# Q, K and V of a 16-head attention: projected token-major and transposed per head by TensorE, with the batch loop written out

## The reference

```python
def _L1_attn_ref(x, Wqkv, Wproj, bproj):
    qkv = jnp.einsum('bnm,fm->bnf', x, Wqkv)          # b=8, n=1024, m=256, f=768
    qkv = qkv.reshape(b, n, N_HEADS, -1)
    q, k, v = (qkv[..., :dh], qkv[..., dh:2 * dh], qkv[..., 2 * dh:])   # dh=16
    scores = jnp.einsum('bnhd,bngd->bnhg', q, k) / SCALE
    attn = jax.nn.softmax(scores, axis=-1)
    out = jnp.einsum('bnhg,bngd->bnhd', attn, v)
    return jnp.einsum('bni,mi->bnm', out.reshape(b, n, -1), Wproj) + bproj
x = L0_attn_x
x = _layernorm(x + _L0_attn_ref(...))
x = _layernorm(x + _L0_ffn_ref(...))
x = _layernorm(x + _L1_attn_ref(...))
x = _layernorm(x + _L1_ffn_ref(...))
```

## Time and profile before

| | us |
|---|---|
| median of 3 runs (lowest, highest) | 1611.36 (1608.79, 1613.42) |
| the profiled execution | 1609.18 |
| its span, first to last instruction | 1607.4 |
| PE, DVE, ACT, POOL busy | 1255.6, 958.1, 669.8, 601.5 |
| mean granted TensorE clock, share of full | 0.837 |
| second transfer queue's total (q1) | 79.93 MB |

### The profile page before, as it was taken

One profiled execution on the slowest core, in us unless ns is written; L12 is line 12 of the kernel. 1 busy time (PEld: TensorE's weight loads), 2 busy tenths in 40 slices (PEclk: granted clock), 3 DMA queues, 4 the chain that ended last, 5 costly groups with the idle time before them and its releaser, 6 DMA issues. The chain is left out here.

```text
span 1607.4 us, 33289 instructions
## 1 busy us (share of the span) xinstructions
PE 1255.6 (78%) x12232; PEld 791.7 (49%) x12232; DVE 958.1 (60%) x2185; ACT 669.8 (42%) x1164; POOL 601.5 (37%) x889
## 2 busy tenths in 40 slices
PE   7689869976998868986898869988789777774452
PEld 4454546543664546553565537545465435531441
DVE  2434666685656747485556756477466866475535
ACT  3322552355432752344623662336523553253423
POOL 2133271344522543335613545324713435243212
PEclk9789977998879977989789887999779886797556
DMA  4000442018120370207320180205520080208220
GB/s 149 14 5 16 102 63 54 15 40 147 16 67 7 95 99 10 59 14 141 47 67 8 66 127 3 66 8 121 72 54 1 27 149 11 54 3 159 24 54 27
DMA packets 92918, 90.78 MB, mean 56 GB/s; under 512 B 7031, under 2 KB 81721, under 8 KB 92474
## 3 DMA queue, kind: packets, MB, share of 16 engines
q1 hardware_dynamic: 90170, 79.93, 25.6%
q0 software_dynamic: 2560, 8.39, 1.5%
HBM read 46.35 MB, written 41.94 MB: 55 GB/s over the span
## 5 line engine op out<-in xcount | busy, mean ns | idle before, releaser
L1430 PE MATMUL bank<-we,at 128*128 128x512 f16 x1536 | 397.3, 423 | 98.0 <-DVE x L1143 49.1
L1430 PEld LDWEIGHTS bank<-we,at 128*128 128x128 f16 x1536 | 161.2, 107 | 317.1 <-issue 126.1
L513 POOL TENSOR_TENSOR part<-part 128x512 f32<-128x512 f32 x64 | 81.2, 1269 | 353.3 <-ACTq L792 353.2
L651 ACT ACTIVATE part<-bank,wexp 128x256 f32<-128x256 f32 x256 | 104.3, 470 | 202.0 <-PE bank L1430 156.9
L768 ACT ACTIVATE x<-x,nm,rs 128x256 f32<-128x256 f32 x192 | 104.4, 593 | 132.5 <-POOL nm L501 132.0
L1143 DVE SCALAR_TENSOR_TENSOR x<-bank,wexp,x 128x256 f32<-128x256 f32 x256 | 122.7, 479 | 56.8 <-PE bank L1430 46.8
L1430 PE MATMUL bank<-bt,wqkv 128*128 128x512 f16 x576 | 138.8, 382 | 20.9 <-DVE stage L985 18.3
L985 DVE TENSOR_TENSOR stage<-bank,stage 128x512 f16<-128x512 f32 x128 | 86.3, 686 | 102.7 <-ACT stage L651 102.7
L651 ACT ACTIVATE blockdiag<-shared,const 128x2048 f16<-128x2048 f16 x64 | 122.7, 1990 | 36.4 <-POOL shared L545 35.6
L651 ACT ACTIVATE stage<-bank 128x512 f16<-128x512 f32 x128 | 75.2, 596 | 125.5 <-PE bank L1430 82.1
L494 POOL TENSOR_SCALAR nm<-mv 128x2 f32<-128x2 f32 x128 | 29.7, 232 | 259.7 <-DVE mv L1020 254.8
(11 more groups left out here) (175 smaller groups left out, 2209.9 us busy)
## 6 DMA issues: line engine op xcount, KB each, us to landing
scratch_qkv<-stage SPq DMA_DIRECT2D x48, 512.0 KB, 3.4
ct<-scratch_qkv SPq DMA_DIRECT2D x128, 128.0 KB, 5.9
x_in<-in_x_dram SPq DMA_DIRECT2D x32, 256.0 KB, 2.7
keys<-scratch_qkv SPq DMA_DIRECT2D x64, 128.0 KB, 10.9
scratch_o<-stage SPq DMA_DIRECT2D x64, 128.0 KB, 3.1
bt<-scratch_o SPq DMA_DIRECT2D x16, 512.0 KB, 3.7
out_dram<-x POOLq DMA_DIRECT2D x32, 256.0 KB, 2.6
blockdiag<-in_expert_w_dram SPq DMA_DIRECT2D x1, 2048.0 KB
```

The costliest lines, as they stand in the source:

```text
L513: pool.tensor_tensor(part[:, 0:2, :], part[:, 0:2, :], part[:, 2:4, :], ALU.add)\
L651: return act.activation(dst, src, ACT.Copy, scale=scale)
L1430: ins = pe.matmul(dst, lhs, rhs, start=(n == 0), stop=(n == len(terms) - 1))
```

## The change

Q, K and V are computed token-major. `b_fqk(b, u)` takes the 128 tokens 8n+u (`x2t`, every eighth column of `bt`) as stationary operand and 512 columns of `wqkv` (Q and K) as moving one, six matmuls; eight of them replace the first eight pieces. `b_fv` does the same for V with 256 columns, twelve matmuls for each of four pairs of tiles. ACT alone copies the fp32 result to SBUF (`qk_tok` in half 1 of `blockdiag`, `v_tok` in `ct`) and frees the bank. Then `b_turn(b, m, j)` transposes four heads of matrix m by TensorE (four fp32 128x128 transposes into one bank), and ACT and DVE split that into operand rows: K straight into `keys`, Q into `bt` (`q_rows`), V into `stage` (`v_rows`). There are 12 such groups in a batch: Q and K at the end of the turn that projects them, V in the next turn between `a_moe` 0, 1 and the first scores. The scratch tensor, its transfers and the four GpSimd copies are gone. The spreads read the new rows. The loops of all five engines are written out for all ten turns.

```diff
-        def f_part(k, part):
-        ...
+        def rows_part(m, j, part):
+            if m == "K":
+                return keys[:, 4 * j:4 * j + 4, P * part:P * (part + 1)]
+            if m == "Q":
+                return q_rows[:, part, :, :, 4 * j:4 * j + 4].rearrange("p c t h -> p h t c")
+            return v_rows[:, part, :, :, 4 * j:4 * j + 4].rearrange("p c u d -> p d (c u)")
+        x2t = bt[:, :, :, :].rearrange("p k l (n u) -> p k l n u", u=T)
# SP: b_f, b_loadq, b_loadk, b_loadv are gone
# POOL
-                pool.tensor_copy(q_rows[hf].rearrange("p (s c) h -> p s c h", c=8),
-                                 compact[:, :, 8 * hf:8 * hf + 8, :]).then_inc(q_turned, 1)
-                pool.tensor_copy(v_rows[hf].rearrange("p (s c) h -> p s c h", c=8),
-                                 compact[:, :, 8 * hf:8 * hf + 8, :]).then_inc(v_turned, 1)
# ACT
-                if k // 2 >= 2:
-                    act.wait_ge(stored[(k // 2) % 2], 48 * b + 16 * (k // 4))
-                copy(f_part(k, HI), f_psum(k)).then_inc(f_hi, 1)
+            def b_fqk(b, u):
+                act.wait_ge(b_full, b_filled(b, f"FQK{u}"))
+                copy(qk_tok[:, :, u, :], b_ps(f"FQK{u}").rearrange("p (m d) -> p m d", d=DH))\
+                    .then_inc(b_free[b_ring(f"FQK{u}")], 1)
+            def b_turn(b, m, j):
+                act.wait_ge(b_full, b_filled(b, f"T{m}{j}"))
+                copy(rows_part(m, j, HI), rows_psum(m, j)).then_inc(turned, 1)
...
                 if c is not None:
-                    b_spreadq(c, slice(0, 5))
+                    b_spreadq(c, slice(0, 3))
                 if b is not None:
                     a_moe(b, 0)
                 if c is not None:
+                    b_turn(c, "V", 0)
+                    b_turn(c, "V", 1)
+                    b_spreadq(c, slice(3, 5))
+                if b is not None:
+                    a_moe(b, 1)
+                if c is not None:
+                    b_turn(c, "V", 2)
+                    b_turn(c, "V", 3)
                     b_spreadq(c, slice(5, T))
# DVE
-                split_lo(f_part(k, LO), f_psum(k), f_part(k, HI)).then_inc(b_free[b_ring(f"F{k}")], 1)
+                split_lo(rows_part(m, j, LO), rows_psum(m, j), rows_part(m, j, HI))\
+                    .then_inc(b_free[b_ring(f"T{m}{j}")], 1)
# PE
+            def b_fqk(b, u):
+                pe.wait_ge(b_free[b_ring(f"FQK{u}")], b_before(b, f"FQK{u}"))
+                if u == 0:
+                    pe.wait_ge(b_free[b_ring("TX3")], b_read(b, "TX3"))
+                sum_of(b_ps(f"FQK{u}"), split_terms(lambda k, i: x2t[:, k, i, :, u],
+                                                    lambda k, j: wqkv[:, j, k, 0:2 * D])).then_inc(b_full, 1)
+            def b_turn(b, m, j):
...
+                for i in range(4):
+                    n = 4 * j + i
+                    if m == "V":
+                        src = v_tok[:, :, :].rearrange("p t (g d) -> p (t g) d", d=DH)[:, :, n]
+                    else:
+                        src = qk_tok[:, H * "QK".index(m) + n, :, :].rearrange("p u d -> p (u d)")
+                    ins = pe.transpose(b_ps(f"T{m}{j}")[:, P * i:P * (i + 1)], src, ident)
+                ins.then_inc(b_full, 1)
...
-                    b_f(b, 10)
+                    b_fv(b, 2)
+                    b_fv(b, 3)
+                    b_turn(b, "Q", 0)
+                    b_turn(b, "Q", 1)
                 if a is not None:
                     a_gate(a)
                 if b is not None:
-                    b_f(b, 11)
+                    b_turn(b, "Q", 2)
+                    b_turn(b, "Q", 3)
                 if a is not None:
                     a_wt(a)
-                    a_bias(a, 0)
...
+                for p in range(TP):
+                    if b is not None:
+                        b_turn(b, "K", p)
+                    if a is not None:
+                        a_bias(a, p)
# every engine
-            with pe.Fori(2, NB) as i:
+            for i in range(2, NB):
                 turn(i, i - 1, i - 2)
```

More of the change, by code:

```diff
@@ L324, in build_two_layer_postln @@
         out_d = out.rearrange("b (t p) d -> b p t d", p=P)
-        q_src, k_src, v_src = [scratch_qkv[D * n:D * (n + 1)].rearrange("(h d) (r n) -> h d r n", d=DH, r=T)
-                               for n in range(3)]
         def places():
@@ L435, in b_loado, with turn @@
                         .then_inc(o_loaded, 16)
-            def turn(a, b, c):
+            def turn(a, c):
                 if c is not None:
@@ L442, in turn @@
                         load_x(a, p)
-                if b is not None:
-                    b_f(b, 1)
-                    b_f(b, 3)
-                    b_f(b, 5)
-                    b_f(b, 7)
-                    b_loadq(b)
-                    b_f(b, 9)
-                    b_loadk(b)
-                    b_f(b, 11)
-                    b_loadv(b)
-            turn(1, None, None)
-            turn(2, 0, None)
-            with sp.Fori(3, NB) as i:
-                turn(i, i - 2, i - 3)
-            turn(None, NB - 2, NB - 3)
-            turn(None, NB - 1, NB - 2)
-            turn(None, None, NB - 1)
-            for s in stored:
-                sp.wait_ge(s, 48 * NB)
+            turn(1, None)
+            turn(2, None)
+            for i in range(3, NB):
+                turn(i, i - 3)
+            turn(None, NB - 3)
+            turn(None, NB - 2)
+            turn(None, NB - 1)
             sp.wait_ge(o_stored, 16 * T * NB)
@@ L969, in turn @@
                 if b is not None:
-                    b_f(b, 11)
+                    b_turn(b, "Q", 2)
+                    b_turn(b, "Q", 3)
                 if a is not None:
                     a_wt(a)
+                if b is not None:
+                    for j in range(4):
+                        b_turn(b, "K", j)
             turn(0, None, None)
             turn(1, 0, None)
-            with act.Fori(2, NB) as i:
+            for i in range(2, NB):
                 turn(i, i - 1, i - 2)
@@ L1417, in _ @@
             turn(1, 0, None)
-            with dve.Fori(2, NB) as i:
+            for i in range(2, NB):
                 turn(i, i - 1, i - 2)
@@ L1764, in turn @@
                     b_tx(b, 3)
-                    b_f(b, 0)
-                    b_f(b, 1)
-                    b_f(b, 2)
-                    b_f(b, 3)
+                    for u in range(4):
+                        b_fqk(b, u)
                 if a is not None:
@@ L1794, in turn @@
                 if b is not None:
-                    b_f(b, 11)
+                    b_turn(b, "Q", 2)
+                    b_turn(b, "Q", 3)
                 if a is not None:
                     a_wt(a)
-                    a_bias(a, 0)
-                    a_bias(a, 1)
-                    a_bias(a, 2)
-                    a_bias(a, 3)
+                for p in range(TP):
+                    if b is not None:
+                        b_turn(b, "K", p)
+                    if a is not None:
+                        a_bias(a, p)
             turn(0, None, None)
             turn(1, 0, None)
-            with pe.Fori(2, NB) as i:
+            for i in range(2, NB):
                 turn(i, i - 1, i - 2)
```

233 lines of the change are left out of this document (83 added, 150 removed).

## The result

The changed kernel takes **1703.76 us** (median of 4 runs, 1703.34 to 1708.25), the kernel before on the same chip 1610.07. The ratio is 1.058, 95% interval 1.056 to 1.061: **slower** by 94 us, where the prediction said 1596.5 us and a range up to 1617. The profiled execution has a span of 1701.5 us and a mean granted clock of 0.817 of full (0.837 before).

What follows compares the result with a forecast made beforehand. No single engine or transfers bound the kernel, but the wait that ends last at each place. Gains of 22.8 us less 8 for scattered writes gave 14.8, 1594.4 us profiled; predicted median 1596.5 us, 8-in-10 range 1566 to 1617.

Steps and rivals of the forecast that it cites:

- Scattered writes: 8 us back: Q and V splits writing single fp16 elements: 0.2 us more on each of 40, a loss of 8 us.
- Rival 3: End of each turn: scattered writes cost ACT and DVE together 0.64 us more a pair; 1618 us, slower; chance 0.20.
- The sum without scattered writes: Whole kernel: loop seams 7.5, loop entry 2.35, seam behind the loop 1.9, last turn 11; 22.8 us of gain.
- No stop at the branch: Loop seams: no PE idle over 2 us with "issue" behind it before the experts' first matmul.
- Spreads 8.8 us in loop turns, 6.1 in turn 8: Turn's start: DVE's eight spreads take 8.8 us beside GpSimd's a_xs, 6.1 without it behind the loop.
- Start of a turn 31.3 us: From DVE's last bias addition to the first transposed probabilities: 31.3 us instead of 36.
- End of a turn 3.2 us longer: From GATE to the last bias addition, GATE later and more DVE splits in the way: 3.2 us longer.
- Loop seams and the one behind, 9.4 us: Five loop seams gain 1.5 us each, 7.5 together; the seam behind the loop gains 1.9.
- Last turn 11 us: Last turn: first transposed probabilities (L1609) near 1493.5 us instead of 1504.83, a gain of 11 us.
- Rival 2: Turn's start: GpSimd holds DVE wholly during a_xs, spreads last 11 us; 1609.5 us, no change; chance 0.12.
- Rival 1: Turn's start is PE's own work, about 24 us instead of 31.3; 1545 us; chance 0.10.
- Rival 4: Branch: the 10 us stop is a fetch that straight code also pays; about 1640 us; chance 0.05.

Runs made afterwards that it cites:

- e12: e1 with V written and read in runs of two fp16 (4 bytes) instead of four, on ACT and DVE; 1595.7 us.
- e8: Changed kernel with ACT in runs of four; DVE's Q split hops only on reads, its V split only on writes; computes something else; 1625.4 us.
- e1: Changed kernel with ACT's copies and DVE's splits of Q and V walking elements in runs of four fp16; 1599.1 us, ratio 0.993.
- e6: e1 with the loops over the batches put back on all five engines; 1614.6 us, ratio 1.002.
- e5: Kernel before with its loops written out and nothing else changed; 1606.6 us, ratio 0.998.
- e7: e1 with GpSimd's four a_xs subtractions moved behind its first two expert sums; 1582.5 us, ratio 0.982.
- e10: e7 with ACT's list reordered: copies of V groups 2 and 3 ahead of the second expert and ACT's fifth spread, last spreads later; 1567.9 us, ratio 0.973.
- e14: e1 plus DMA traffic that computes nothing, 12 writes of 512 KB from each batch's first Q group on; 1595.7 us.

## Why the prediction was wrong

**The step that failed is "Scattered writes: 8 us back".** It put 0.2 us on each of 40 splits and 25.6 us as the far end for both engines. Measured are 1.67 us on a DVE split, 1.76 on an ACT copy, and 104.7 us in all: 2.6 us for each of the 40. The price failed: a split's is eight times what I took and five times its far end, 0.34. The count of 40 fits only on the mean. Its 32 Q pairs are worth 69.4 us, 2.2 each, but its 8 V pairs 35.3, 4.4 each, more than the 3.43 of a whole pair, so more than one V split of a batch was on the path. Which of the others, no run shows. Two choices made the price so low. The low end came from rows in runs of four, which I took for nearly the same thing; by e12 even runs of 4 bytes are free, and single fp16 are a different case. The high end came from POOL, whose copy hops on the read side; e8 shows that the read costs 0.33 us and the write the rest. That row bounded the wrong side of the instruction. A number without a near row wants a range as wide as the ignorance, and this one fed 40 instructions on two engines.

**Rival 3 was the right mechanism**, with its point of decision (0.57 us a pair) and, for Q's 69.4 us, its place at the end of each turn; V's 35.3 us fall at the start. Its price of 0.64 a pair was 3.43 in truth. With 40 pairs at that price its sum would give some 1726 us in place of 1618; 1703.8 were measured, as ACT's and DVE's pieces overlap in part. One of the signs named ahead also came: Q splits over 1.2 us. The third, slower projections, did not: their matmuls of 512 columns take 388 ns on the mean against 382.

The other terms can be read in e1, where only that step is taken out. The sum without scattered writes was 22.8 us of gain. e1's median lies 11.3 us below before's; its profiled execution, the fastest of its four, 16.1 by span. In the profiled pair:

- *No stop at the branch: held* (nothing over 1.39 us on PE). But that the stop was a matter of the loop alone was half the story: without the trip of Q, K and V it would have been 2 us (e6). And e5 shows that its removal alone is worth 3.8 us.
- *Spreads 8.8 us in loop turns, 6.1 in turn 8:* 8.41 in the kernel after, 8.21 in e1, 5.38 in turn 8. Held in kind. The free value, 6.09 us, was read from V's spreads, of which one took 1.55 us beside a GpSimd normalisation of 1.41 us, so it was not free; that made up for a cost of GpSimd's copy that was put too low (2.7 us, where 8.80 less 5.38 are 3.4).
- *Start of a turn 31.3 us:* 32.1 in e1 at the loop's seams and at the entry (208.32 to 240.45), 26.4 behind the loop, where 28.6 was said. `a_moe` 2 took 7.83 at a granted clock of 0.67, so the clock did not come back. The sum hides a term that was too low: `a_moe` 1 was put at 5.4 and took 6.99 at a granted clock of 0.76, behind an idle time of 4.52 us. In e7, behind 1.70 us, it takes 5.35 at full clock:

```profile
770.40 6.99 PE L1357 MATMUL bank<-we,at 128*128 128x512 f16 x24 [4.52 <-DVE x L1082]
```

```profile
764.57 5.35 PE L1357 MATMUL bank<-we,at 128*128 128x512 f16 x24 [1.70 <-DVE x L1082]
```

- *End of a turn 3.2 us longer:* on the mean of the loop a turn of e1 lasts 184.3 us where it was 184.8, with a start shorter by 3.6, so the rest is 3.1 longer. Held in the loop. At the entry it failed: the last bias addition ends at 208.32, not 201.16, 7.2 us later. The projection already starts 2.2 us later, 1.50 of it behind the fourth transposed tile, and between `WT` and the last bias addition another 3.2 come in. There the first probabilities come 2.4 us later instead of 2.35 earlier.
- *Loop seams and the one behind, 9.4 us:* from the first probabilities of turn 2 to those of turn 8 1100.4 us instead of 1107.0: 6.7, where 9.4 was said.
- *Last turn 11 us:* L1609 of the last turn stood 159.8 us behind that of turn 8, in e1 149.1 us (1340.82 to 1489.94). 10.7: held.

-2.4 + 6.7 + 10.7 and 1.2 behind the last are the 16.1. **Rival 2** (GpSimd holds DVE wholly) falls by its size: 5.86 us of GpSimd cost 2.83, not 4.9. Its mechanism is right for each instruction by itself. The Trainium skill, SBUF — State Buffer, section Terms, has the ports locked for a full instruction and the loser fully blocked meanwhile; the trace agrees, with a spread of 0.74 us that takes 1.64 beside a subtraction and 4.10 beside the copy (e7, above). The prediction doubted this because it added up whole streams; between two GpSimd instructions DVE gets one of its own through. **Rival 1** was 0.10 and did not come, but the way to it was open: e7 and e10 take the start of the turn from 32.1 to between 26.2 and 27.1 us, near its 24. **Rival 4** falls with e1 and e14.

## What to carry to other kernels

Before an instruction writes 16-bit results with a step, look at how many bytes lie side by side at its destination, and make the walk's innermost dimension those elements, even if PSUM must then be read with hops. It costs nothing to write and was worth 105 us here. Do not sum a stall as a gain before asking what is late next: the 49 us of stops in the kernel before were worth 3.8 us alone (e5), and what did pay was to move a GpSimd stream away from DVE's (17 us) and to place ACT's pieces behind the ones that others wait for (15 us).

## What the runs showed of the hardware

- Writes of single fp16 at steps of 32 and of 256 bytes cost DVE and ACT the same, 2.36 us for 512 a partition, 4.6 ns each; in runs of 4 or 8 bytes 0.65 to 0.69 and 0.53 to 0.60. Reads of single fp16 from SBUF took a DVE split from 0.69 to 1.02 us; reads from PSUM in steps of 512 bytes added nothing.
- The queues named "instruction" (q8, q14) share the DMA engines with data. A loop's branch stopped PE and DVE for 1.9 to 2.4 us on idle engines, 4.6 to 6.0 us beside 337 GB/s of traffic, 8.8 to 10.5 in the kernel before. Written-out code was not stopped by the same traffic.
- A DVE `tensor_scalar` of 128x2048 fp16 takes 0.74 us alone and stands while a GpSimd instruction on SBUF runs: it ended 0.55 us behind a subtraction of 1.60 us and 0.54 behind a copy of 3.64. The subtraction takes 1.17 us alone. Eight in a row take 5.38 us alone, 8.21 beside four subtractions, and 12.37 beside a copy and four subtractions (e5).
- A load of PE's stationary operand, 128x128 fp16, takes 96 ns when it is contiguous and 143 at steps of 16 bytes (V's and Q's projections in e1). No run shows that this reached the time.
